# Another order of the products in each turn of the first attention, with the other engines' orders to match

## The reference, cut to what matters

```
x = x + tanh(g_xattn[0]) * xattn(layernorm(x), ctx, ...)
# in xattn, per sample of 8 (256 tokens, 256 context rows, width 512, 16 heads of 32):
q = rms_norm(x @ q_w.T + q_b, norm_q_w)
k_img = rms_norm(ctx @ k_img_w.T + k_img_b, norm_k_img_w)
v_img = ctx @ v_img_w.T + v_img_b
img_x = softmax(q @ k_img.T / sqrt(32)) @ v_img      # per head
out = img_x @ o_w.T + o_b
```

## Time and profile before

| | us |
|---|---|
| median of 3 runs | 2386.82 |
| lowest, highest | 2385.69, 2395.93 |
| profiled execution | 2392.47 |
| its span, first to last instruction | 2390.8 |
| PE busy in the span | 2202.5 (92%) |
| DVE, ACT, POOL busy | 1380.9 (58%), 1006.5 (42%), 858.9 (36%) |
| first attention, turns 0 to 7 | from 60.87 to about 445 |

### The profile page before, as it was taken

The page is one execution under the profiler, slowest core; times in us unless marked ns, Lnnn a source line. Parts: engine busy times, 40 slices in busy tenths (PEclk is TensorE's granted clock), DMA queues, the critical chain, the costliest instruction groups (busy, mean ns, idle before and its releaser), DMA issues. The chain is left out here.

```text
span 2390.8 us, 41820 instructions
## 1 busy us (share of the span) xinstructions
PE 2202.5 (92%) x17133; PEld 1803.1 (75%) x17150; DVE 1380.9 (58%) x2370; ACT 1006.5 (42%) x1782; POOL 858.9 (36%) x729
## 2 busy tenths in 40 slices
PE   5888898588979999999999999999889999899995
PEld 4666666344458888898899999998777777789994
DVE  7778886488874344433443345444454545677776
ACT  4776532377743223222332223222245453435552
POOL 3323332366532222222322232332245453135543
PEclk9999999899989999999999999999989999999998
DMA  6454102100021102111111112110000000147766
GB/s 246 159 170 140 54 2 106 53 1 1 1 80 63 36 27 80 71 36 36 60 42 68 36 41 82 36 45 19 23 2 2 2 2 28 72 176 280 287 231 233
DMA packets 44829, 186.90 MB, mean 78 GB/s; under 512 B 6368, under 2 KB 6368, under 8 KB 38240
## 3 DMA queue, kind: packets, MB, share of 16 engines
q1 hardware_dynamic: 37600, 161.16, 18.8%
q0 software_dynamic: 7040, 23.07, 2.8%
HBM read 153.80 MB, written 30.41 MB: 77 GB/s over the span
## 5 line engine op out<-in xcount | busy, mean ns | idle before, releaser
L247 POOL TENSOR_TENSOR c_prob<-c_prob,c_inv_mass 128x512 f32<-128x512 f32 x128 | 130.4, 1040 | 437.9 <-DVE c_inv_mass L239 437.9
L229 ACT ACTIVATE c_prob<-c_s_ps,c_neg_peak 128x256 f32<-128x256 f32 x256 | 117.8, 473 | 360.5 <-DVE c_neg_peak L218 360.5
L47 PE MATMUL c_ring<-bc_xt_lo,bc_wq_hi 128*128 128x256 f32 x512 | 151.8, 297 | 5.4 <-POOL bc_xt_lo L1672 5.4
L47 PE MATMUL c_ring<-c_ctx_lo,c_w_hi 128*128 128x256 f32 x512 | 146.3, 286 | 0.0
L48 PE MATMUL c_ring<-bc_xt_hi,bc_wq_hi 128*128 128x256 f32 x512 | 145.9, 285 | 0.0
L49 PE MATMUL c_ring<-bc_xt_hi,bc_wq_lo 128*128 128x256 f32 x512 | 145.9, 285 | 0.0
L49 PE MATMUL c_ring<-c_ctx_hi,c_w_lo 128*128 128x256 f32 x512 | 143.1, 280 | 0.0
L48 PE MATMUL c_ring<-c_ctx_hi,c_w_hi 128*128 128x256 f32 x512 | 143.0, 279 | 0.0
L1676 POOL TENSOR_TENSOR c_ctx_lo<-c_ctx_f,c_ctx_hi 128x1024 fp32r<-128x1024 f32 x32 | 78.3, 2447 | 166.9 <-ACT c_ctx_hi L1865 166.9
L525 POOL TENSOR_TENSOR a_fold<-a_prob 128x1024 f32<-128x1024 f32 x32 | 76.3, 2385 | 158.1 <-ACT a_prob L841 156.4
L1672 POOL TENSOR_TENSOR bc_xt_lo<-c_xt_f,bc_xt_hi 128x1024 fp32r<-128x1024 f32 x32 | 79.1, 2471 | 128.4 <-ACT bc_xt_hi L1859 128.4
(11 more groups left out here) (545 smaller groups left out, 7110.9 us busy)
## 6 DMA issues: line engine op xcount, KB each, us to landing
x_res<-b_w SPq DMA_DIRECT2D x48, 512.0 KB, 4.5
e_raw<-e_w SPq DMA_DIRECT2D x15, 1536.0 KB
bc_raw<-c_w SPq DMA_DIRECT2D x16, 1024.0 KB, 5.9
c_ctx_f<-ctx_t SPq DMA_DIRECT2D x32, 512.0 KB, 3.5
c_xt_f<-xnt_scratch SPq DMA_DIRECT2D x24, 512.0 KB, 3.3
h_res<-e_w SPq DMA_DIRECT2D x8, 1536.0 KB
wq_scratch<-x_res SPq DMA_DIRECT2D x24, 256.0 KB, 2.7
ab_wq<-wq_scratch SPq DMA_DIRECT2D x3, 2048.0 KB, 12.7
```

The costliest lines, as they stand in the source:

```text
L47: pe.matmul(out, lhs[0], rhs[1], start=first, stop=False)
L229: ins = act.activation(self.prob[:, u % 2, j, 0:w], self.s_ps[:, j, 0:w], ACT.Exp, bias=self.neg_peak[:, u % 2, j:j + 1], scale=self.scale ...
L247: pool.tensor_tensor(part, part, self.inv_mass[:, u % 2, js].unsqueeze(2).to_broadcast([P, 2, w]), ALU.mult).then_inc(self.prob_done, 1)
```

## The change

PE's order in a turn becomes: `turn_peaks`, `turn_x(i+1, 0)`, v0, TS0, `turn_x(i+1, 1)`, q0, TS1, w0, q1, TS2, w1, m0, v1, TS3, w2, and from kt0 on as before. `PLACES` follows. DVE has the first query bias and `scale_keys` ahead of the second value bias, does all query work ahead of `invert(i, 0)` and the second value, and both low parts of the keys after that. ACT has both squares of the queries ahead of the third exponentials, the context's high part behind them, and the weight pieces at other places. POOL has the context's low part between folds 2 and 3. Turn -1 has the old order of products.

```
-    PLACES_OF_STEPS = {-1: (0, 2, 1, 1, 2), 0: (2, 4, 2, 4, 6), 1: (1, 2, 1, 3, 4), 2: (1, 2, 1, 2, 3), 3: (0, 1, 0, 1, 2)}
+    PLACES_OF_STEPS = {-1: (0, 2, 1, 1, 2), 0: (2, 1, 1, 6, 8), 1: (1, 0, 1, 4, 5), 2: (1, 0, 1, 3, 4), 3: (0, 0, 0, 2, 2)}
...
-        PLACES = (("mt", 0), ("xt0", 1), ("v0", 1), ("xt1", 1), ("v1", 1), ("q0", 1), ("m0", 0), ("q1", 1), ("kt0", 1),
+        FIRST_PLACES = (("v0", 1), ("v1", 1), ("q0", 1), ("q1", 1))
+        PLACES = (("mt", 0), ("mean", -1), ("xt0", 1), ("v0", 1), ("xt1", 1), ("q0", 1), ("q1", 1), ("m0", 0), ("v1", 1), ("kt0", 1),
...
-            await_ready(sp, "q1", BATCH - 1)
+            await_ready(sp, "v1", BATCH - 1)
```

On POOL:

```
+                if i == -1:
+                    context_low(i + 2)
                 if here(i):
                     fold_keys(i, 0)
                     fold_keys(i, 1)
                 if i >= -1 and here(i + 2):
-                    context_low(i + 2)
-                if i >= -1 and here(i + 2):
                     add_row(i + 2)
                 if here(i):
                     fold_keys(i, 2)
+                if i >= 0 and here(i + 2):
+                    context_low(i + 2)
+                if here(i):
                     fold_keys(i, 3)
```

On PE:

```
             def queries(s, t):
-                if t == 0:
-                    await_free(pe, "xt0", s)
-                    await_free(pe, "xt1", s)
+                await_free(pe, f"xt{t}", s)
...
-                if now:
-                    turned_scores(i, 0)
                 if nxt:
                     values(i + 1, 0)
                 if now:
-                    turned_scores(i, 1)
+                    turned_scores(i, 0)
                 if i >= 0 and nxt:
                     turn_x(i + 1, 1)
...
+                if nxt:
+                    queries(i + 1, 0)
+                if now:
+                    turned_scores(i, 1)
                     weigh(i, 0)
                 if nxt:
-                    values(i + 1, 1)
-                    queries(i + 1, 0)
+                    queries(i + 1, 1)
                 if now:
                     turned_scores(i, 2)
                     weigh(i, 1)
                     masses(i, 0)
-                if nxt:
-                    queries(i + 1, 1)
+                if i >= 0 and nxt:
+                    values(i + 1, 1)
```

On ACT:

```
                     exponentials(i, 0)
-                next_weights(i, 0)
...
                     exponentials(i, 1)
-                if i >= -1 and here(i + 2):
-                    context_high(i + 2)
-                next_weights(i, 1)
                 if nxt:
                     square_query(i + 1, 0)
+                    square_query(i + 1, 1)
                 if now:
                     exponentials(i, 2)
                     output_raw(i, 0)
-                if nxt:
-                    square_query(i + 1, 1)
+                next_weights(i, 0)
+                if i >= 0 and here(i + 2):
+                    context_high(i + 2)
                 if now:
                     exponentials(i, 3)
+                if i >= 0:
+                    next_weights(i, 1)
                 if nxt:
                     keys_high(i + 1, 0)
                     keys_high(i + 1, 1)
-                next_weights(i, 2)
-                if nxt:
                     queries_high(i + 1, 0)
                     queries_high(i + 1, 1)
+                next_weights(i, 2)
```

On DVE:

```
                     key_scales(i + 1)
+                if i == -1:
                     value(i + 1, 1)
                     scale_keys(i + 1)
+                if nxt:
                     query(i + 1, 0)
+                if i >= 0 and nxt:
+                    scale_keys(i + 1)
                 if i >= -1 and after:
                     normalise(i + 2)
-                if now:
-                    invert(i, 0)
                 if nxt:
                     query(i + 1, 1)
                     query_scales(i + 1)
+                    scale_queries(i + 1)
+                if now:
+                    invert(i, 0)
+                if i >= 0 and nxt:
+                    value(i + 1, 1)
+                if nxt:
                     low("kt", i + 1, 0, kt_lo, kt_hi, kt_hi_done)
-                    scale_queries(i + 1)
                     low("kt", i + 1, 1, kt_lo, kt_hi, kt_hi_done)
```

More of the change, by code:

```diff
@@ L394, in image_attention @@
         for i in TURNS:
[L395 to L398, removed]
+            for name, ahead in (FIRST_PLACES if i == -1 else ()) + PLACES:
+                if here(i + ahead) and (name, i + ahead) not in use_of and (name != "mean" or i == 1):
                     use_of[name, i + ahead] = len(use_of)
@@ L730, in _ @@
                 if now:
-                    turned_scores(i, 1)
+                    turned_scores(i, 0)
                 if i >= 0 and nxt:
                     turn_x(i + 1, 1)
+                if i == -1:
+                    values(i + 1, 1)
+                    pe.wait_ge(w_lo_done[WQ], 1)
+                if nxt:
+                    queries(i + 1, 0)
                 if now:
+                    turned_scores(i, 1)
                     weigh(i, 0)
                 if nxt:
-                    values(i + 1, 1)
-                    if i == -1:
-                        pe.wait_ge(w_lo_done[WQ], 1)
-                    queries(i + 1, 0)
+                    queries(i + 1, 1)
                 if now:
```

1 line of the change is left out of this document (added).

## The result

The changed kernel takes 2430.74 us (median of 4 runs, 2428.5 to 2432.98) against 2389.94 (4 runs of the kernel before on the same chip, 2385.69 to 2395.93). The ratio is 1.0169, 95% interval 1.0142 to 1.0196: slower by some 40 us. The profiled execution took 2430.44, its span is 2428.7, 37.9 more than the span before. One execution of a later run (all three repairs, 6736.64 us against 2380.84 to 2393.54 for the other nine) counts in that run's median and is left out of its ratio.

The account below looks back on a forecast made before the run. TensorE was taken to set the pace, its waits being what the change could win. The terms summed to +22.4 us on the profiled 2392.5, giving 2415, less 5.7 to the median: 2409 us, range 2382 to 2429.

Parts of the forecast that it names:

- the sum: Whole kernel: all terms added make it 22.4 us slower; chance 0.55, own range 2396 to 2424.
- The steady turn: Turns 4 and 5: second key transpose waits for the reciprocal, S0 at T+34.3; 2.6 us longer each, +5 in all.
- rival A: Query chain is through before fold 2; waits for scaled queries and exponentials go: -13 us, 2374; chance 0.13.
- The clock: Turns 4 and 5: longer idle stretch lowers TensorE's clock; 1 us a turn, bounds 0 and 3, +2 in all.
- Rival C: Turns 0 to 5: gaps of 5 us or more, each with 3 us at half rate behind; +36, 2423; chance 0.12.
- The low end of the sum: All unknown terms at their low ends (clock 0, means 1.7, turn 3 0, steady turns 0): +9 us, 2396.
- The weight pieces: Turns 0 to 2: ScalarE's pieces ahead of the output's high part delay the outputs' first product; +2, +4.6, +3.2 us.
- The means: Head of turn 1: product of the means waits for ScalarE's magnitudes of turn 0; 3 us, bounds 1.7 and 5.3.
- Turn 3: Late weight pieces delay the load of sample 5, q1 at T+16.6 instead of T+10.8; +6 us, 0 if pieces keep up.
- Turn 4: Replayed as a steady turn: 2.6 us longer, plus 1 for the clock; 3.5 in the forecast by turn.
- Turn 2 and the small terms: Turn 2: S0 at T+35.4 against T+37.1, -1.7, with pieces +1.5 us; turn 6: -2; turn -1: +0.3.
- The scaling of the queries: Turns 0 to 2: VectorE's query scaling taken as held beside GpSimd's context low, S0 at T+32.3; otherwise T+30.4.

Follow-up runs that it names:

- all three repairs: Kernel after with GpSimd held until the queries are scaled, the first reciprocal ahead of the query chain, and the old table of places: 2386.64 us, ratio 0.9986.
- the fill: Kernel after with twenty unused matmuls ahead of the second key transpose in turns 3 to 5: 2431.37 us, ratio 1.015.
- The kernel after with the wait: Kernel after with GpSimd waiting behind fold 2 until the queries are scaled, then fold 3, then the context's low part: 2404.41 us, ratio 1.0076.
- The swaps: Table of places exchanged: the old table in the kernel after, 2409.4 us; the new table in the kernel before, 2415.73 us.

## Why the prediction was wrong: 2409 forecast, 2431 measured

The side was right and the size too small; the time lies 1.7 us above the range. Of the 21.5 us between forecast and median, 15.5 are the sum (22.4 forecast, 37.9 in the spans). The other 6.0 have nothing to do with the change: the prediction took 5.7 off, the distance of the profiled execution before from its median, while the profiled execution after was 0.3 under its own.

**The steady turn, right.** TensorE's wait ends with `a_inv_mass`, 5.92 to 6.1 in turns 3 to 5 (about 6 forecast), at T+30.0 (30.2). The key scaling is held (3.05 under fold 1), the second query bias ends at T+17.0 as replayed (368.64 with 0.68), the chain at T+27.3 (27.65). The sum gave this wait to turns 4 and 5 alone, though turn 3 has it too (6.05). S0 was forecast at T+34.3; it comes at 35.7, and at exactly 34.3 where the fill keeps the clock up. That the chain would end no earlier although its product comes 5.8 earlier was the heart of the argument, and rival A (the relay wins) fell with it. The kernel after with the wait shows that in turns 4 and 5 GpSimd's operations kept A from coming true (46.9 in turn 5 against 49.3 before). On the whole time they weren't alone: with the wait it is still 2404, not 2374.

**The clock, the step that failed.** I charged it 1 us in each of turns 4 and 5 and nothing elsewhere; measured, the lower clock made TensorE busy for 11.6 us more. In turns 4 and 5 PE is busy only 0.7 and 0.2 longer than before, since the old order had its own slow stretch behind the 2.65 us wait. In turns 0 to 3, where I had put nothing, it is 2.5 + 3.7 + 1.5 + 3.3 = 11 us. It is found at two places. In turns 0, 1 and 2 the long wait for `a_o_lo`, which I had foreseen for turns 1 and 2, stands right ahead of a projection of twelve matmuls. That projection took 5.46, 4.94 and 4.61 us, against 2.98 to 3.02 before, and from its start to the turn's end it is 9.5, 8.6 and 8.3, against 6.7 to 6.8: 6.2 us more. The other place is the stretch from the second key transpose to S0. It took 6.0 us in turns 0, 1 and 3, and 4.3 in turn 2, as in turns 3 to 5 of the run with work in the idle stretch (4.27): 1.7 us each time. PE's row of turn 0 of the kernel after:

```profile
110.38 0.77 PE L47 MATMUL a_ring<-a_w_lo,a_o_hi 128*128 128x512 f32 x1 [3.85 <-issue]
```

The first matmul takes 0.77 there, as at the lower level, 1.2 GHz, in the earlier trace rows. A wait that the sum contains should have brought its clock with it in every turn. Rival C did so, in all of turns 0 to 5, and at 2423 came nearest. That is luck in part: its 14 us were near the 11.6 measured, but its gap of 5 us or more in every turn isn't there (turn 0 has 3.85 at the most, turn 2 3.20), and by its own terms, 3 us in six turns less the 2 of the sum, it should have said 16, and 2425. The low end of the sum, too, is +8 by its terms and not +9.

**TensorE's waits in turns 0 and 1.** The prediction had S0 at T+32.3 there, and called that within 0.3 of before; it was 34.0 and 32.8 before and is 35.4 and 35.2 after. Besides the clock, TensorE waits 2.6 for the last exponentials in both turns and then 1.8 and 1.5 for the reciprocal, and the sum has neither. The exponentials come late because the weight piece of place 0 and the context's high part now stand ahead of them on ScalarE (turn 1: from 141.15 to 144.5, the exponentials from 144.43). This is what the rows show; no run moved those two.

**The weight pieces, right in turns 1 and 2.** The outputs' first product was forecast at S0 + 15.4 and + 13.1 and came at + 15.3 and + 12.9, with waits of 5.65 and 3.20. In turn 0 the delay was 2.6, not 2. The means cost 1.43, under the low bound of 1.7; I had taken 3. The swaps put the cost of the table at 21 to 26. The prediction's terms for pieces were 2 + 3 + 4.6 + 3.2 + 6 = 18.8, or 17 with the 1.7 that turn 2 should win. For the order some 4 to 5 are left of its sum, where the swaps gave 15 to 18: what the order costs in turns 0 to 3 is the larger part of the miss.

**Turn 3, too small by 4.3.** I let the pieces end 6.8 us into the turn and the loss come through the load of sample 5. They end 9.4 into it. ACT at the head of turn 3 of the kernel after:

```profile
243.75 1.24 ACT L870 ACTIVATE x_res<-x_res,a_shifts,a_inv_mean 128x1024 f32<-128x1024 f32 x1 [2.21 <-DMA x_res<-b_w]
245.03 1.15 ACT L872 ACTIVATE x_res<-x_res,a_shifts 128x1024 bf16<-128x1024 f32 x1
246.08 0.36 ACT L803 ACTIVATE a_peak_t<-a_ring 128x256 fp32r<-128x256 f32 x1
```

ACT works in order, so the turned maxima wait behind the last piece and with them the first turned scores, which go at T+9.8 after 5.69 idle. That is a shorter way to the loss than the load, and I hadn't followed it. The load came late too (statistics at T+13.9, after 3.08 of DMA wait; forecast 12.5), but sample 5's wait wasn't the longest, as I had said it would be: sample 4's was 4.43.

**Turn 4, too small by 1.3.** One more piece reached into it: ACT's piece at 298.13 waited 3.73 for its DMA, so `a_peak_t` came 2.2 into the turn and the second key transpose at T+31.4. With the old table it goes at T+30.0 in turn 4 as well. I had taken turn 4 for free of pieces, as it was before. The old table in the new order has no such late piece, and the steady loss of turn 4 is then 3.2 for 3.5 forecast.

**Turn 2 and the small terms.** S0 of turn 2 came at T+36.6, 0.5 earlier than before and not 1.7: q1 waited 2.73 for the second low part of x (T+15.1, forecast 13.7). Turn 6 won 1.6 (2), turn -1 lost 0.6 (0.3).

**The scaling of the queries.** The prediction named the Trainium skill ("GPSIMD Engine Reference", key points) for the scaling of the queries: with one SBUF input it contends with GpSimd by that rule when it runs in a two-port mode, and no row showed whether it does. The trace after has the row, DVE in turn 0:

```profile
86.06 2.99 DVE L993 TENSOR_SCALAR a_qf<-a_qf,a_q_rstd 128x512 f32<-128x512 f32 x2
```

2.99 for the pair, against 0.88 where GpSimd is idle. By that rule, the trace agrees, and I had taken "held".

## What to carry to other kernels

Before small VectorE steps on SBUF are moved earlier, look at when GpSimd's last operation next to them ends: here that set their end, and whatever was queued behind them on VectorE paid. One wait that keeps GpSimd back until the chain is through was worth 12 us in the old order and 26 in the new. And each idle stretch that a forecast adds should be charged with its clock in every turn, above all where a long product follows it; work given to an in-order engine at the end of a turn is also work ahead of the next turn's head.

## What the runs showed of the hardware that I had not expected

- In these turns VectorE's TENSOR_TENSOR, SCALAR_TENSOR_TENSOR and TENSOR_SCALAR with all operands in SBUF were held under a GpSimd operation, the integer TENSOR_SCALAR on 128x2 among them (2.29 at 293.15 in the kernel before with GpSimd's new order, against 0.17). Instructions with an operand in PSUM weren't: reciprocal 1.75, bias 0.62 to 0.69. Nor was BATCH_NORM_STATS2, though it reads SBUF (0.68 at 251.35 in the kernel after, under a fold). GpSimd's own operations took 2.34 to 2.41 whether a VectorE step was held or not; only where the scaling of the queries ran as they began did they take more (2.52 to 2.61, four times in turns 0 to 2 of the kernel after).
- The clock comes back wholly in turn 5: with 1.9 us of idle ahead of the second key transpose in place of 5.9 the granted clock of the whole turn was 1.00, with 5.9 it was 0.93, and with twenty useless matmuls in the gap 1.00 again, worth 1.5 us.
- What stays open: how much of the 11 us of turns 0 to 3 the whole time would get back. Those turns are read from one execution each, turns 0 to 2 differed by 2.8 us in sum between two executions of the same instructions, and no run filled the wait for `a_o_lo`.
